# Quantised attention and routed experts on one core: the softmax sum unscaled, q clipped in two pieces, weights split by ScalarE and VectorE

## What is computed

```python
def fake_quant(q, s, z):
    zr = round(z)
    return s * (clip(round(q / s) + zr, 0.0, 15.0) - zr)

h = patches @ proj_w + proj_b                              # 768 -> 192
qkv = fake_quant(layernorm(h)) @ fake_quant(ww1).T         # 192 -> 3 x 768
dots = einsum('bhnd,bhmd->bhnm', fake_quant(q), fake_quant(k)) * 64 ** -0.5
a = softmax(dots)
out = einsum('bhnm,bhmd->bhnd', fake_quant(a, sa, za), fake_quant(v))
h = h + fake_quant(out) @ fake_quant(ww2).T + bb2
x = layernorm(h)
top = argmax(x @ Wg + bg)                                  # 4 experts
h = h + (gelu(x @ W1[top] + b1[top]) @ W2[top] + b2[top])
```

## Time and profile before

| what | us |
|---|---|
| median of 3 runs | 204.62 |
| lowest, highest | 203.27, 205.04 |
| the profiled execution | 204.57 |
| its span, first to last instruction | 202.7 |
| TensorE busy in it | 148.3 |
| VectorE busy | 150.2 |
| ScalarE busy | 120.6 |
| GpSimd busy | 86.4 |

### The profile page before, as it was taken

One profiled execution on the slowest core, in us unless ns is written; L12 is line 12 of the kernel. 1 busy time (PEld: TensorE's weight loads), 2 busy tenths in 40 slices (PEclk: granted clock), 3 DMA queues, 4 the chain that ended last, 5 costly groups with the idle time before them and its releaser, 6 DMA issues.

```text
span 202.7 us, 5048 instructions
## 1 busy us (share of the span) xinstructions
PE 148.3 (73%) x1794; PEld 113.5 (56%) x1794; DVE 150.2 (74%) x434; ACT 120.6 (60%) x228; POOL 86.4 (43%) x115
## 2 busy tenths in 40 slices
PE   0687897198768999899566758519731799999960
PEld 0786786144544556566344547419520688888840
DVE  3175768768999998999999934589902568989880
ACT  8933682179987789789846671950520255656620
POOL 2022212963996568356738211238850103132332
PEclk9999999679995555859955555557995599999997
DMA  4799801999922012001200400003257901000000
GB/s 138 298 267 296 324 3 12 353 216 284 357 56 101 0 21 100 0 3 19 101 0 3 123 0 0 0 10 131 91 186 176 364 28 31 24 27 24 23 23 20
DMA packets 9463, 21.45 MB, mean 106 GB/s; under 512 B 1744, under 2 KB 5210, under 8 KB 9440
## 3 DMA queue, kind: packets, MB, share of 16 engines
q1 hardware_dynamic: 8288, 18.17, 29.7%
q0 software_dynamic: 1152, 2.97, 4.0%
HBM read 15.39 MB, written 6.04 MB: 106 GB/s over the span
## 4 chain that ended last, share of the span: by engine, by line
PE 33%; DVE 22%; issue 12%; DMA 10%; ACT 9%; POOL 7%; SPq 4%; DVEq 0%; POOLq 0%; ACTq 0%
PE lin_bank L1112 9%; DMA patches<-in_patches 7%; PE head_bank L1124 5%; POOL slots L421 5%; PE lin_bank L910 3%; ACT oint L520 3%; PE head_bank L1131 2%; DMA patches<-slots 2%; PE score_bank L984 2%; ACT vint L464 2%; DVE oT L593 2%; ACT qkint L472 2%; PE head_bank L883 2%; PE lin_bank L914 2%; DVE dens L722 2%
## 5 line engine op out<-in xcount | busy, mean ns | idle before, releaser
L556 ACT ACTIVATE q<-lin_bank,b 128x128 f32<-128x128 f32 x72 | 25.2, 367 | 34.2 <-PE lin_bank L1112 32.9
L1112 PE MATMUL lin_bank<-q,w 128*128 128x128 f16 x360 | 31.2, 226 | 1.0 <-DVE q L824 1.0
L1112 PEld LDWEIGHTS lin_bank<-q,w 128*128 x360 | 25.0, 101 | 4.9 <-issue 1.7
L427 POOL DMA_INDIRECT out<-q,patches x12 | 11.6, 969 | 37.2 <-DVE q L847 36.9
L520 ACT ACTIVATE oint<-head_bank,fac 64x432 int16<-64x432 f32 x32 | 19.7, 616 | 7.9 <-PE head_bank L967 7.5
L1124 PE MATMUL head_bank<-early,q 128*128 x72 | 22.9, 336 | 0.4 <-DVE q L865 0.3
L914 PE MATMUL lin_bank<-xqT,ww1q 96*128 96x288 bf16 x96 | 19.5, 351 | 1.4 <-ACT qkint L472 0.7
L883 PE MATMUL head_bank<-proj_w,patches 128*128 128x192 f32 x72 | 14.2, 354 | 8.3 <-DMA patches<-in_patches 8.3
L933 PE MATMUL score_bank<-k,q 128*128 128x36 bf16 x256 | 9.8, 188 | 13.4 <-DVE dif L707 8.9
L392 POOL TENSOR_SCALAR patches<-patches 128x768 f32<-128x768 f32 x8 | 17.5, 2189 | 4.9 <-DMA patches<-in_w 4.8
L472 ACT ACTIVATE qkint<-lin_bank,fac 128x576 int16<-128x576 f32 x24 | 17.2, 739 | 4.1 <-PE lin_bank L914 3.6
(11 more groups left out here) (135 smaller groups left out, 347.6 us busy)
## 6 DMA issues: line engine op xcount, KB each, us to landing
patches<-in_patches SPq DMA_DIRECT2D x9, 384.0 KB, 11.9
slots<-blank SPq DMA_DIRECT2D x12, 226.0 KB, 9.3
patches<-slots SPq DMA_DIRECT2D x12, 226.0 KB, 4.7
patches<-in_w SPq DMA_DIRECT2D x4, 576.0 KB, 4.0
early<-in_ww SPq DMA_DIRECT2D x3, 576.0 KB, 11.1
patches<-in_w SPq DMA_DIRECT2D x1, 1536.0 KB, 8.5
patches<-in_w SPq DMA_DIRECT2D x2, 768.0 KB, 12.7
proj_w<-in_proj_w SPq DMA_DIRECT2D x1, 576.0 KB, 4.3
```

The lines of the kernel that those rows point to most:

```text
L556: a.activation(g[:, j % 2, m], up_bank[n % 4][:, 0:P], ACT.Gelu, scale=1.0 / WSCALE, bias=b1[:, bass.ds(e, 1), m]).then_inc(g_ok, 1)
L1112: last = mm(up_bank[n % 4][:, 0:P], up_weights(j, part, m), xT[:, j % 3, piece], start=x == 0, stop=x == len(PASSES) - 1)
```

## The change

- `dens` is gone: `rden` is the reciprocal of `den` itself, and the product for `aint` takes the inverse scale of a as a scalar from memory.
- q gets a buffer `qint` of its own, laid out in the order in which q is used. The linears of q take head pairs n and n+3 instead of 2n and 2n+1, ScalarE writes each in runs of 36, and VectorE clips a chunk in two instructions of 64x1728 (one for each half of the partitions) instead of four of 64x864.
- `attend` takes one head's 64 columns of v as stationary operand and writes them to the lower or upper 64 output partitions, so that both heads of m lie in one block of 36 columns; `oint` is one instruction of 128x432 for a pair. Waits on `o_int` and `q_ok` count accordingly.
- GpSimd splits nothing. All 16 pieces are made as `split_high` on ScalarE and `split_low` on VectorE, inside the loop: w1's highs at the end of ScalarE's steps 6 to 13, w2's at the end of steps 15 to 22; the low stands at the end of VectorE's step after (the last behind the loop).

```diff
+        qint = sb("qint", [P, G3, CI, TRI, NTOK], I16)
+        kint = sb("kint", [P, HB, CH], I16)
...
+        def splits_at(i):
+
+            return [n for n in range(len(SPLITS)) if i == (6 + n if n < EARLY else 7 + n)]
...
-            pool.wait_ge(w1_in, 48)
-            split(0)
-            split(1)
             for t in range(TT):
-                if t + 2 < EARLY:
-                    split(t + 2)
...
+                a.activation(qint[:, :, :, n], bank[:, :, 0:CH].rearrange(
+                                 "p g (i n) -> p g i n", n=NTOK), ACT.Copy, scale=rq).then_inc(lin_int, 1)
...
-                    for hp in range(2):
-
-                        rows = slice(DH * hp, DH * hp + DH)
-                        a.activation(dst[rows].rearrange("p m (r n) -> p r m n", r=2),
-                                     head_bank[rows, :, 0:HT].rearrange("p r (m h n) -> p r m h n", m=HB, h=2)[:, :, :, hp],
-                                     ACT.Copy, scale=ro[rows]).then_inc(o_int, 1)
+                    a.activation(dst.rearrange("p m (r n) -> p r m n", r=2),
+                                 head_bank[:, :, 0:HB * NTOK].rearrange("p r (m n) -> p r m n", m=HB),
+                                 ACT.Copy, scale=ro).then_inc(o_int, 1)
...
+                for n in splits_at(i):
+                    split_high(n)
...
-            for n in range(EARLY, len(SPLITS)):
-                split_high(n)
...
-                    for g in range(G3):
-                        for upper in range(2):
-                            rows = slice(DH * upper, DH * upper + DH)
-                            clip(q_slots[rows, c % 2, g, :, upper:upper + 11:5], qkint[rows, TRI * g:TRI * (g + 1)].rearrange(
-                                     "p t (i n) -> p i t n", n=NTOK), QQ, DH, DH * upper).then_inc(q_ok, 1)
+                    for upper in range(2):
+                        rows = slice(DH * upper, DH * upper + DH)
+                        clip(q_slots[rows, c % 2, :, upper:upper + 11:5], qint[rows].rearrange("p g i t n -> p (g i) t n"),
+                             QQ, DH, DH * upper).then_inc(q_ok, 1)
...
-                if old:
-                    dve.wait_ge(den_ok, p + 1)
-                    d.tensor_scalar(dens[0:TR, ob], den[0:TR, ob], scl[0:TR, AQ:AQ + 1], None,
-                                    ALU.mult).then_inc(dens_ok, 1)
...
-                    d.tensor_tensor(groups(aint[0:TR, ob]), groups(ex[0:TR, ob]),
-                                    rden[0:TR, ob].unsqueeze(2).to_broadcast([TR, SG, NTOK]),
-                                    ALU.mult).then_inc(aint_ok, 1)
+                    d.scalar_tensor_tensor(groups(aint[0:TR, ob]), groups(ex[0:TR, ob]), inv[0:TR, AQ:AQ + 1],
+                                           rden[0:TR, ob].unsqueeze(2).to_broadcast([TR, SG, NTOK]),
+                                           ALU.mult, ALU.mult).then_inc(aint_ok, 1)
...
+                for n in splits_at(i - 1):
+                    split_low(n)
+            for n in splits_at(STEPS - 1):
+                split_low(n)
...
             for j in range(PICKED):
-                for n in range(j * rest // PICKED, (j + 1) * rest // PICKED):
-                    split_low(EARLY + n)
                 slots_T(j)
...
-                            m = 2 * n + half + (HB if kind == "k" else 0)
+                            m = HB + 2 * n + half if kind == "k" else n + QG * half
...
-                            last = mm(head_bank[:, par, h * NTOK:(h + 1) * NTOK],
-                                      v[rows, p % VB, m * P:(m + 1) * P],
+                            last = mm(head_bank[DH * hp:DH * hp + DH, par, m * NTOK:(m + 1) * NTOK],
+                                      v[rows, p % VB, h * DH:(h + 1) * DH],
                                       aT[rows, p % 2, h * NTOK:(h + 1) * NTOK], start=True, stop=True)
```

More of the change, by code:

```diff
@@ L139, in vit_kernel @@
         den = sb("den", [P, 2, SG])
-        dens = sb("dens", [P, 2, SG])
         rden = sb("rden", [P, 2, SG])
@@ L219, in vit_kernel @@
         lin_ps, lin_int, q_ok, k_ok, v_ok = map(sem, ("lin_ps", "lin_int", "q_ok", "k_ok", "v_ok"))
-        s_ps, mx_ok, dif_ok, ex_ok, den_ok, dens_ok, rden_ok, aint_ok, aq_ok = map(sem, (
-            "s_ps", "mx_ok", "dif_ok", "ex_ok", "den_ok", "dens_ok", "rden_ok", "aint_ok", "aq_ok"))
+        s_ps, mx_ok, dif_ok, ex_ok, den_ok, rden_ok, aint_ok, aq_ok = map(sem, (
+            "s_ps", "mx_ok", "dif_ok", "ex_ok", "den_ok", "rden_ok", "aint_ok", "aq_ok"))
         aT_ps, aT_ok, o_ps, o_int, o_ok = map(sem, ("aT_ps", "aT_ok", "o_ps", "o_int", "o_ok"))
@@ L466, in linear @@
                     return
-                m = 2 * n
+                if c >= 1 and n == 0:
+                    act.wait_ge(q_ok if kind == "q" else k_ok, 2 * c if kind == "q" else c)
                 if kind == "k":
[L469 to L473, removed]
+                    a.activation(kint[:, 2 * n:2 * n + 2], bank[:, :, 0:CH], ACT.Copy, scale=rk).then_inc(lin_int, 1)
+                    return
+                a.activation(qint[:, :, :, n], bank[:, :, 0:CH].rearrange(
+                                 "p g (i n) -> p g i n", n=NTOK), ACT.Copy, scale=rq).then_inc(lin_int, 1)
             def split_high(n):
-                act.wait_ge(w2_in[SPLITS[n][1]], 16)
+                if n < EARLY:
+                    act.wait_ge(w1_in, 48)
+                else:
+                    act.wait_ge(w2_in[SPLITS[n][1]], 16)
                 w, whi, _ = split_views(n)
@@ L644, in linear @@
                         dve.wait_ge(s_ps, (c - 1) * PPC)
-                    clip(k[:, c % 2], qkint[:, HB:2 * HB], KQ).then_inc(k_ok, 1)
+                    clip(k[:, c % 2], kint[:], KQ).then_inc(k_ok, 1)
                 else:
@@ L658, in split_low @@
                 dve.wait_ge(whi_ok, n + 1)
-                d.scalar_tensor_tensor(wlo, w, WSCALE, whi, ALU.mult, ALU.subtract).then_inc(wlo_ok, 1)
+                rows = slice(TAIL if SPLITS[n][0] == 1 and SPLITS[n][2] else 0, P)
+                d.scalar_tensor_tensor(wlo[rows], w[rows], WSCALE, whi[rows], ALU.mult, ALU.subtract).then_inc(wlo_ok, 1)
             for t in range(TT):
@@ L717, in _ @@
                     n //= 2
[L718 removed]
+                    dve.wait_ge(o_int, 2 * n + 2)
                     clip(oT[:, :, n * 4 * NTOK:(n + 1) * 4 * NTOK], oint[:, n % 2], X2).then_inc(o_ok, 1)
[L720 to L723 removed]
                 clipped = clips_of(i - 1) if i else []
@@ L728, in _ @@
                 if old:
-                    dve.wait_ge(dens_ok, p + 1)
-                    d.reciprocal(rden[0:TR, ob], dens[0:TR, ob]).then_inc(rden_ok, 1)
+                    dve.wait_ge(den_ok, p + 1)
+                    d.reciprocal(rden[0:TR, ob], den[0:TR, ob]).then_inc(rden_ok, 1)
                 if old:
                     dve.wait_ge(rden_ok, p + 1)
-                    d.tensor_tensor(groups(aint[0:TR, ob]), groups(ex[0:TR, ob]),
-                                    rden[0:TR, ob].unsqueeze(2).to_broadcast([TR, SG, NTOK]),
-                                    ALU.mult).then_inc(aint_ok, 1)
+                    d.scalar_tensor_tensor(groups(aint[0:TR, ob]), groups(ex[0:TR, ob]), inv[0:TR, AQ:AQ + 1],
+                                           rden[0:TR, ob].unsqueeze(2).to_broadcast([TR, SG, NTOK]),
+                                           ALU.mult, ALU.mult).then_inc(aint_ok, 1)
                 for x in values[1:]:
@@ L920, in scores @@
                 if r == 0:
-                    pe.wait_ge(q_ok, 4 * c + 4)
+                    pe.wait_ge(q_ok, 2 * c + 2)
                     pe.wait_ge(k_ok, c + 1)
@@ L957, in attend @@
                 if p >= 1:
-                    pe.wait_ge(o_int, 2 * p)
+                    pe.wait_ge(o_int, p)
                 for m in range(HB):
@@ L1049, in _ @@
                 for t in tiles_at(i, 4):
-                    pe.wait_ge(o_int, 2 * min(i - 1, PAIRS))
+                    pe.wait_ge(o_int, min(i - 1, PAIRS))
                     gate(t)
```

9 lines of the change are left out of this document (3 added, 6 removed).

## The result

The changed kernel takes 194.43 us (median of 4 runs, 193.62 to 195.36), the kernel before 204.83 beside it: a ratio of 0.951, interval 0.946 to 0.957. So it is 10.4 us faster, where 7.8 was forecast. The profiled execution took 194.78 us around a span of 193.0.

The account below looks back on a forecast made before the run. VectorE was taken to bound the attention loop, with ScalarE or TensorE almost as full in places. Loop 4.1, drain 0.2 and scatter 3.5 sum to 7.8 us: 204.57 - 7.8 = 196.8 us, range 192.5 to 200.5 (own range 195.0 to 198.5).

Parts of the forecast that it names:

- first rival: Loop: VectorE stays the bound, TensorE takes nothing back, its clock mostly at the higher level; 194.8 us, chance 0.18.
- Stalls of aq, oT and xn: VectorE in the loop: stalls of 3.2, 2.2 and 2.2 us go, with aint's 0.8 together 8.4 us.
- The sum 8.0: VectorE's load in steps 2 to 15 falls by 6.2 + 8.4 + 1.1 - 0.7 - 7.0 = 8.0 us.
- Taken back by TensorE, 2.0: Loop: TensorE, nearly full at its lower clock, takes back 2.0 us of VectorE's gain; bounds 0 and 5.
- The loop, 4.1: Attention loop gets shorter by 8.0 - 1.9 - 2.0 = 4.1 us.
- ScalarE bounds steps 2 to 4: Loop: VectorE gains 4.1 us there, but full ScalarE lets the three steps shorten by only 2.2, taking 1.9 back.
- ScalarE level in the steps with highs: Steps 6 to 13: the 0.62 us saved per eviction pair stands against one w1 high of 0.8 us.
- Drain +0.2: Drain after the loop: two evictions gain 1.2 us, the w2 splits cost 1.0, so 0.2 us gained.
- Scatter 3.5: Scatter: without VectorE's lows, the ninth indirect, the loads and tile 3 come 3.5 us earlier; bounds 0 and 3.9.
- attend unchanged: TensorE's 24 attend products in the new shape: no change in time taken; bounds 0.27 and 1.6 us.
- q's slow mode: Rival: q's 1728-element clips on VectorE cost 1.3 ns a column, 2.2 us each; 202.9 us, chance 0.04.
- the lock of the splits: Rival: lows wait for ScalarE's highs, stalling VectorE 1.5 us in each of eight steps; 208.8 us, chance 0.04.

Follow-up runs that it names:

- experiment 6: The changed kernel with the scaling of the softmax sum (dens) put back and the aint product with two operands: 195.15 us, ratio 0.951.
- experiment 1: The changed kernel run and profiled once more, unedited: 195.54 us, ratio 0.951 to the kernel before.
- experiment 3: The changed kernel with the eight w2 splits back at the scatter, as in the kernel before; w1's stay in the loop: 195.40 us, ratio 0.952.
- run 7: The changed kernel with the w2 splits spread over places where ScalarE and VectorE sat idle: 193.78 us, ratio 0.945.
- run 9: The changed kernel once more, unaltered, on the third chip: 193.61 us, ratio 0.948.
- run 10: The changed kernel with the w2 splits in idle places of ScalarE and VectorE, once more on the third chip: 193.37 us, ratio 0.942.
- run 4: The changed kernel with four extra two-tensor instructions and four reductions on VectorE beside the scatter, results unread: executed once, 195.20 us.
- run 8: The kernel of run 7 plus 70 and 50 extra unread matmuls to keep TensorE's clock up: 198.45 us, ratio 0.968.
- run 12: The changed kernel with four extra three-operand and five one-tensor instructions on VectorE beside the scatter, results unread: executed once, 192.58 us.
- run 11: The kernel of run 10 with the slots of tile 3 loaded second: 192.42 us, ratio 0.940.
- experiment 5: The changed kernel with attend's pair products and the two evictions a pair as in the kernel before: 197.87 us, ratio 0.965.

## Why the prediction held, and where its steps did not

The time lies in the range given, 192.5 to 200.5, just below the forecast's own 195.0 to 198.5 and nearest to the first rival's 194.8. What was to become shorter did; that the sum came so near owes something to luck, as errors in the loop cancelled. The steps one by one:

- **Stalls of aq, oT and xn**: gone as said. VectorE's groups in steps 2 to 15 lost 6.5 (dens), 3.3 (aq), 2.2 (oT), 2.1 (xn) and 1.1 us (q), gained 7.6 (lows) and, its stall set off, 0.1 (aint, 0.06 each). A stall of v's clips, 0.7 us (523 ns to 474), had been missed. No run put q's four clips back by themselves, so its 1.1 us is read from durations alone.
- **The sum 8.0** was too high: VectorE's busy time fell by 63.76 - 57.47 = 6.3 us. The durations above give 8.2. Durations of neighbours overlap on the timeline: over all of VectorE's instructions in the stretch by 10.4 us before and 8.6 after. With 11 instructions fewer at some 0.09 us each, that is 1.0 us; and one stall of 0.7 was counted twice, in a dens and in the clip of v behind it:

```profile
78.70 0.89 DVE L722 TENSOR_SCALAR dens<-den,quant 108x8 f32<-108x8 f32 x1
78.83 0.96 DVE L593 TENSOR_SCALAR v<-vint,lo,hi 128x768 bf16<-128x768 int16 x1
```

  Of the single terms, dens' own work would be 2.7 us by the starts of experiment 6 (seven at 0.26, seven at 0.13) and not 3.1, and the w1 lows took 0.95 us each and not 0.88.
- **Taken back by TensorE, 2.0**, was wrong: it was 0 to 0.9. Mx of pair 5 to 15 takes 45.43 us in experiment 1 and 45.42, 45.42, 45.42 and 45.41 in runs 3, 7, 9 and 10, at a granted clock of 0.78 or 0.79, with TensorE 10.6 us free. It takes 45.8 in runs 4, 8 and 12 and 46.3 in the first profile and in run 11, at 0.71 to 0.75; single steps are longer there, the others equal to 0.01 us. The granted clock did what the rival had said: 0.63 before, 0.80 after, over steps 5 to 11.
- **The loop, 4.1**: 65.87 - 61.87 = 4.0 us in the first profile, where the errors above cancelled. That execution is the longest but one of its kind: mx of pair 2 to 15 takes 58.46 us in it (62.31 before), 57.27 in experiment 1 and 56.36 in run 9, which is 5.0 and 5.9 us shorter than before. The first rival's 8.0 - 1.9 = 6.1 fits these better than 4.1.
- **ScalarE bounds steps 2 to 4**: right, 2.0 us came where 2.2 were forecast, and up to 3.2 in runs whose granted clock from 38 to 48 us was 0.70 or more. In those ScalarE is full, as in run 9 (columns as in the earlier trace rows):

```profile
47.69:58.63 10.94, 10.21 (x198) 6.56 (x195) 9.63 (x27) 10.89 (x20) 0.00 (x0) 1.00 0.83 280
```

- **ScalarE level in the steps with highs**: right, and worth more than the sentence made of it. With the second eviction and the old products those steps are 2.2 us longer (experiment 5).
- **Drain +0.2**: 0.3 measured from step 16 to logit (16.31 to 15.99). Cost of the w2 splits 1.3 for 1.0.
- **Scatter 3.5**: 4.0. The fifth and the fourth stall were sized well; those of the second and sixth indirect (1.08 and 1.32 us for 0.97) had been left out. That the time falls by as much is not shown: with the lows put back, tile 4 was only 1.8 us later after the first indirect, and the total the same (experiment 3).
- **Behind the scatter** nothing was forecast, and 1.0 us came: 0.4 until the scatter landed, 0.7 as tile 2 ran at the higher clock. The second profile has the opposite sign (3.63 and 11.68 us for 2.74 and 10.70), so this part belongs to the execution. Between the two profiled executions the forecast was 1.9 us short: 0.1 in the drain, 0.5 in the scatter, 1.0 here, 0.3 at the start. Another 0.7 lies between that and the medians. Its cause isn't shown; the loop alone differs by up to 2.1 us between executions of this kernel (58.46, 57.27, 56.36). Three sets of runs gave 0.951, 0.951 and 0.948.
- **attend unchanged**: a gain of 0.03 to 0.10 us a pair, no loss. The rule of the Trainium skill, TensorEngine Tiling (Array Packing), section Restrictions, that column tiling switches fast weight load off, would have made it dearer; here the 24 products take 0.37 us for 0.47, so if the loads of weights were slower, it is more than made up for. Whether they were no run here shows apart.
- **q's slow mode and the lock of the splits** did not come. VectorE's idle time ahead of the w1 lows is 0.1 us at most. The sum in that last rival was off: with its own 7.8 + 2.0 to lose first, eight stalls of 1.5 us give 206.8 and not 208.8.

## What to carry to other kernels

Compare an instruction's median with its minimum: where GpSimd works beside VectorE, the difference can be a stall, and moving GpSimd's work pays most in the stretches in which VectorE has nothing to take over. Price what is removed by the distance between starts, not by durations: a dens shown as 0.22 us was worth 0.26 or 0.13, by what stood behind it. An engine that takes over work needs its room made first: here one eviction instead of two, with its products, paid for the highs, and without them a quarter of the gain was gone. A stretch that gets shorter isn't yet time gained: of the scatter's 4.0 us, 1.8 were left by tile 4 (experiments 1 and 3). And profile the same kernel more than once before reading a difference of 1 or 2 us.

## What the runs showed of the hardware that I had not expected

- A plain two-tensor instruction of VectorE holds GpSimd's indirect up as much as a three-operand one (2.71 and 2.70 us for 0.97), a reduction not at all (0.98), one-tensor instructions from float32 to float16 a little (1.20).
- VectorE's lows also stretch GpSimd's small pow for rstd: its mean went from 592 to 963 ns. At 72.97 one took 1.28 us beside a low that ran from 72.89 to 73.85. In most steps nobody waited for it.
- TensorE's last products for the picks and its first for tile 0 came in pieces, with pauses of 0.3 to 1.2 us in which it waited for nothing that the profile shows, until the scatter had landed. They are in the first profile of the changed kernel and in all eight of the second and third chip, in none of the four of the first, and not in that of the kernel before. Tile 2 then ran at a granted clock of 1.00 in all nine (3.15 to 3.53 us), and at 0.58 to 0.66 in the five without them (4.65 to 5.29 us), where TensorE had sat idle. What they are is open; that they end with the scatter's landing speaks for something that TensorE fetches by DMA, and that is argued only.
